# The S5 output of a hybrid layer, made with tokens on partitions and its skip term as a diagonal matmul

## The chip, the core and the metric

The kernel runs on one core of a Trainium2 chip. The time is device time in microseconds for one execution; given are the median of three runs and, for reading, one execution taken with the hardware profiler.

The core's engines are named as in the profile: PE is TensorE (PEld its weight loads), DVE is VectorE, ACT is ScalarE, POOL is GpSimd, SP issues most of the DMAs. Each runs its own instructions in order and waits on semaphores for the others.

## What is computed

Input `x` is 8 batches of 512 tokens with 128 features, all in float32. Four blocks follow each other, each with a layer norm ahead and a residual: a selective state-space block (S6, 256 inner channels with 64 states each), a mixture of experts (8 experts, top 2), an S5 block, and the same mixture of experts again. The change lies in the S5 block:

```python
Lambda_bar = jnp.exp(Lambda * step)
B_bar = ((Lambda_bar - 1.0) / Lambda)[:, None] * B_tilde
Bu = jnp.einsum('blh,ph->blp', u.astype(jnp.complex64), B_bar)
_, xs = jax.lax.associative_scan(combine, (A, Bu), axis=1)
ys = jnp.einsum('blp,hp->blh', xs, C_tilde).real + D * u
...
x = x + _L0_attn_b_ref(_layernorm(x, axis=-1), ...)
```

`u` is the normalized input, `D` one skip factor for each of the 128 features, and there are 64 complex states.

## The kernel before

The kernel handles one batch of 512 tokens at a time. The costly part is S6: 256 channels by 64 states are 128 tiles of 128 rows by 512 tokens. For each tile ACT makes a decay `da` (line 837), POOL the product `w` (line 947, two tiles at a time), DVE runs the scan `h` (line 1251), and PE sums the states (line 633, four tiles at a time). `da` has a ring of 2 pairs, `w` of 5, `h` of 6, so each engine can be only so far ahead of the next.

A **turn** is 128 slots, one scan each. Into the scans of batch b every engine weaves other work at slots written out by hand in `PE_STEPS`: `pre` (norm and projections of batch b+1), `post` (S6's output, the first mixture, S5 and the beginning of the second mixture of batch b-1) and `late` (the rest of the second mixture of batch b-2). Within a slot the scan's work comes first, then `late`, `post`, `pre`. A step's lag behind its PE slot is written with it on each engine. The first pass makes batch 0 ready, then there are eight turns, and a last pass without scans for what is left over. In the text they are counted from 0: turn 0 has no `post`, turn 7 no `pre`.

Three PSUM banks H, G and Y serve all the woven work. A step claims its bank by waiting until the one before it in that bank was drained.

S5 of one batch goes through these steps; all tiles have features, states or tokens on the 128 partitions:

- `uT`, slot 83: the normalized tokens are transposed on PE and copied to `nT` (features by tokens).
- `P1`, `P2`, slot 85: two matmuls of 512 columns into H and Y. DVE turns them by cosine and sine, scans (line 1220), and turns them back into `zt[0]` (line 1223, slot 89) and `zt[1]` (line 1225, slot 90), which are states by tokens and which the trace calls `tq`. The second drains P2.
- `s5`, slot 92, bank H: two matmuls (lines 611 and 613) with the output matrices `mc` as the stationary operand and `zt` as the moving one give features by tokens. The first starts once `zt[0]` is there.
- The skip, slot 93 on DVE (line 1228): `nT` times the feature's factor `sdt` plus the bank, into `yT`, which the trace calls `sq`. It drains s5.
- `s5t`, slot 95, bank Y: four transpositions back to tokens by features; at slot 96 DVE adds them to `x1` into `x2` (line 1233); at slot 97 the moments for the last norm follow (lines 1097 and 1100).

Beside this the next batch's projections run: `dt1`, slot 94 (line 521), goes into bank H. ACT takes it at slot 97 (lines 750 and 751), and after a table load an exponential and a logarithm (lines 754 to 759) DVE makes `dl` from it (line 1120, slots 100 and 101), which SP stores and loads back spread out for the next turn.

Of the kernel before, what the change touches and what calls it, by code (L numbers as in the profile page):

```python
# [91 lines left out]
def weigh_slot(m, e, n):  # L92
# [12 lines left out]
MATRICES_AT = PRE_AT + 11  # L105
TURN_AT = PRE_AT + 18
SCALE_AT = 52
LN_AT = [PRE_AT - 6, 7, 16, S5_AT, MOE_AT[2] - 8]
RSTD_LAG, NORM_LAG = 6, 6
ROUTE = 14  # L110
FIRST_LOADS, PROJECTION_LOADS, LATE_LOADS, EXPERT_LOADS = 6, 13, 12, 3
# [4 lines left out]
PE_STEPS = [  # L116
    (5, "post", "Y", "z"), (MOE_AT[1] - 2, "post", "Y", "x1T"), (MOE_AT[1], "post", "Y", "lg1"),
    (S5_AT + 6, "post", "Y", "uT"), (S5_AT + 8, "post", "H", "P1"), (S5_AT + 8, "post", "Y", "P2"),
    (S5_AT + 15, "post", "H", "s5"), (S5_AT + 18, "post", "Y", "s5t"),
    (MOE_AT[2] - 2, "post", "Y", "x3T"), (MOE_AT[2], "post", "Y", "lg2"),  # L120
] + [(PRE_AT + _n, "pre", _b, _name) for _n, _b, _name in (
    (0, "H", "xnT"), (2, "G", "in0"), (3, "H", "in1"), (7, "G", "in2"), (8, "H", "in3"), (11, "G", "stepsB"),
# [100 lines left out]
def hybrid_kernel(nc, x, Wi, bi, Wx, bx, Wdt, bdt, A_log, Dp, Wo, bo, gamma, beta, Lre, Lim, SB, SC, SD, log_step,  # L223
# [3 lines left out]
    with ExitStack() as ctx:  # L227
        def sb(name, shape, dt=F32):
            return ctx.enter_context(nc.sbuf_tensor(name, shape, dt))
# [15 lines left out]

        s5p = sb("s5p", [128, 3]); s5w = sb("s5w", [128, 32]); s5i = sb("s5i", [128, 1], I32)
        mb = sb("mb", [128, 2, 128]); mc = sb("mc", [128, 2, 128])
        cosT = sb("cosT", [128, L]); sinT = sb("sinT", [128, L]); rT = sb("rT", [128, L]); sdt = sb("sdt", [128, 1])

        xnew = sb("xnew", [128, TT, D]); xn = sb("xn", [128, TT, D]); xnT = sb("xnT", [128, L])  # L250
        th = sb("th", [128, 2, L]); vh = sb("vh", [128, 2, L]); spa, du, dl = th, th, vh
# [12 lines left out]
        sbt, sct = z[0:NS, 0:2, :].rearrange("p a c -> p (a c)").rearrange("p (h j) -> p h j", j=2), z[:, 2, :].rearrange("p (n j) -> p n j", j=2)  # L264
        bb, cc = nrm[0:NS, :, :], x1[:, 0:2, :].rearrange("p j (c n) -> p j c n", c=2)
        zt = [tq[:, 0, :], tq[:, 1, :], sq[:, 0, :], sq[:, 1, :]]
        yT = zt[2]

        banks = {n: ctx.enter_context(nc.psum_tensor("bank" + n, [128, 512], F32)) for n in "HGY"}
        da = [ctx.enter_context(nc.psum_tensor(f"da{j}", [128, 2, 512], F32)) for j in range(D_RING)]  # L270
# [180 lines left out]
        def _(pe):  # L451
# [5 lines left out]
            def is_filled(t, name, ins):  # L457
                ins.then_inc(filled[BANK[name]], 1)

            def turn_tiles(t, name, src):  # L460

                p = claim(t, name)
                for a in range(TT):
                    ins = nc.tensor.transpose(p[:, a * 128:(a + 1) * 128], src(a), ident[:, :])
                is_filled(t, name, ins)
# [117 lines left out]
            def post(t):  # L583
                c = t.b - 1
                yield SLOT["z"]
                p = claim(t, "z")
                pe.wait_ge(direct_ready, 2 * c + 2)
                for a in range(TT):
                    for k in range(2):
                        nc.tensor.matmul(p[:, a * 128:(a + 1) * 128], xd[:, k, a * 128:(a + 1) * 128], wo[:, k, :],  # L590
                                         start=(a == 0 and k == 0), stop=False)
                pe.wait_ge(ys_taken, 2 * c + 2)
                for a in range(TT):
                    for k in range(2):
                        ins = nc.tensor.matmul(p[:, a * 128:(a + 1) * 128], y3[:, k, a * 128:(a + 1) * 128], wo[:, k, :],
                                               start=False, stop=(a == TT - 1 and k == 1))
                is_filled(t, "z", ins)
                yield from moe(t, 1, False)
                yield SLOT["uT"]
                pe.wait_ge(normed[3], 4 * c + 4)  # L600
                turn_tiles(t, "uT", lambda a: nrm[:, a, :])
                yield SLOT["P1"]
                for k, name in enumerate(("P1", "P2")):
                    p = claim(t, name)
                    if k == 0:
                        pe.wait_ge(drained[BANK["uT"]], t.before("uT") + 1)
                    is_filled(t, name, nc.tensor.matmul(p[:, :], mb[:, k, :], nT[:, :], start=True, stop=True))
                yield SLOT["s5"]
                p = claim(t, "s5")
                pe.wait_ge(real_ready, c + 1)  # L610
                nc.tensor.matmul(p[:, :], mc[:, 0, :], zt[0], start=True, stop=False)
                pe.wait_ge(drained[BANK["P2"]], t.before("P2") + 1)
                is_filled(t, "s5", nc.tensor.matmul(p[:, :], mc[:, 1, :], zt[1], start=False, stop=True))
                yield SLOT["s5t"]
                pe.wait_ge(drained[BANK["s5"]], t.before("s5") + 1)
                turn_tiles(t, "s5t", lambda a: yT[:, a * 128:(a + 1) * 128])
                yield from moe(t, 2, False)

            def late(t):
# [336 lines left out]
        def _(v):  # L956
# [11 lines left out]
            def link(ins):  # L968

                step[0] += 1  # L970
                ins.then_inc(setup_chain, 1)
# [34 lines left out]
            def diagonal_setup():  # L1006
# [66 lines left out]
                while n < L:  # L1073
# [10 lines left out]
                    c_, c_next, s_, s_next = c_next, c_, s_next, s_  # L1084
                    n *= 2
                link(V.tensor_scalar(rT[:, :], cosT[:, :], 0.0, er, ALU.mult, ALU.add))
                v.wait_ge(matrices_turned, 1)
                link(V.tensor_copy(mb[:, :, :].rearrange("p n c -> p (n c)"), banks["Y"][:, 0:256]))
                link(V.tensor_copy(mc[:, :, :].rearrange("p n c -> p (n c)"), banks["Y"][:, 256:512]))
# [101 lines left out]
            def post(t):  # L1191
# [31 lines left out]
                V.tensor_tensor(zt[0], p2[:, :], cosT[:, :], ALU.mult).then_inc(real_ready, 1)  # L1223
                yield SLOT["P1"] + 5
                drain("P2", V.tensor_tensor(zt[1], p2[:, :], sinT[:, :], ALU.mult))
                yield SLOT["s5"] + 1
                p = got(t, "s5")
                drain("s5", V.scalar_tensor_tensor(yT[:, :], nT[:, :], sdt[:, 0:1], p[:, :], ALU.mult, ALU.add))
                yield SLOT["s5t"] + 1
                p = got(t, "s5t")  # L1230
                if not known(c, 1):
                    v.wait_ge(x_out, 16 * c)
                drain("s5t", V.tensor_tensor(flat(x2), flat(x1), p[:, :], ALU.add))
                v.wait_ge(drained[BANK["s5t"]], t.before("s5t") + 1)
                yield from moments(4, c, LN_AT[4], x2)
                yield from both(moe_tiles(t, 2, False), routing(t, 2))

# [55 lines left out]
```

## Time and profile before

| | before |
|---|---|
| median of 3 runs | 1848.97 us (1846.12 to 1856.43) |
| the profiled execution | 1861.63 us |
| its span, first to last instruction | 1859.7 us |
| mean granted PE clock | 0.860 of 2.4 GHz |
| scan instructions of DVE (line 1251) | 1024 |

The profiled execution is one more run of the same program, and its times are those of the rows. A row of the timeline gives the start, the duration, the engine, line, operation and tiles, how many instructions it merges, and in brackets how long the engine stood idle before it and what released it. A PE row's end is modelled and can lie behind the start of the next row. The granted clock is 1.0 at 2.4 GHz and 0.5 at 1.2 GHz.

### The profile page before, as it was taken

What the parts mean: (1) busy time and instruction counts of PE and PEld (TensorE: products, weight loads), DVE (VectorE), ACT (ScalarE), POOL (GpSimd) and SP (SyncE); (2) the same over time, 40 slices, a digit from 0 to 9 for tenths busy, and PEclk for the clock granted to TensorE, in tenths of its full rate; (3) what the DMA queues carried; (4) which work ended last, traced back from release to release, by engine and by line L of the source; (5) the groups of instructions that cost most, each with busy time, mean ns of one, the idle gap of its engine ahead of it and who ended that gap; (6) DMA issues with size and microseconds to landing.
All of it is one profiled execution on the core that took longest, in us unless ns stands there. A gap on an engine that the chain in (4) does not pass through costs nothing.

```text
span 1859.7 us, 19053 instructions
## 1 busy us (share of the span) xinstructions
PE 1351.0 (73%) x5928; PEld 617.7 (33%) x5928; DVE 1514.5 (81%) x2105; ACT 1281.5 (69%) x2275; POOL 1513.9 (81%) x888
## 2 busy tenths in 40 slices
PE   4336458777886887778776878778787778668958
PEld 1001123234342343324342343324332343324535
DVE  4879988898889889898899888888888988895222
ACT  4547668687877778777777778777787777755423
POOL 0899999978998799977998899987998799983312
PEclk9557569889987989879897989879898898979979
DMA  3601411122111311132101401132111321100000
GB/s 87 212 34 71 164 46 51 49 91 97 57 40 48 148 51 33 54 104 96 55 25 50 162 29 51 49 106 81 51 51 49 102 85 52 46 29 1 7 1 6
DMA packets 38747, 121.89 MB, mean 66 GB/s; under 512 B 5875, under 2 KB 21110, under 8 KB 26358
## 3 DMA queue, kind: packets, MB, share of 16 engines
q1 hardware_dynamic: 37062, 120.67, 18.3%
q8 instruction: 47, 0.77, 0.2%
q14 instruction: 54, 0.44, 0.1%
q10 hardware_dynamic: 1584, 0.01, 0.0%
HBM read 109.13 MB, written 11.53 MB: 65 GB/s over the span
## 4 chain that ended last, share of the span: by engine, by line
PE 27%; ACT 18%; DVE 15%; POOL 14%; issue 8%; DVEq 0%; POOLq 0%; ACTq 0%
DVE h L1251 10%; POOL w L947 9%; PE bankH L565 8%; ACT da L837 5%; PE bankY L579 5%; PE bankG L565 5%; ACT yk L798 4%; ACT L837 3%; PE ys L633 2%; POOL x L890 2%; PE bankG L512 2%; DVE aq L1189 1%; PE bankY L559 1%; ACT L785 1%; ACT sq L785 1%
## 5 line engine op out<-in xcount | busy, mean ns | idle before, releaser
L1251 DVE TENSOR_TENSOR_SCAN h<-da,w 128x512 f32<-128x512 f32 x1024 | 1192.1, 1206 | 158.3 <-ACT da L837 133.0
L947 POOL TENSOR_TENSOR w<-ur,br 128x1024 f32<-128x1024 f32 x512 | 1193.6, 2365 | 33.1 <-DVE h L1251 21.2
L837 ACT ACTIVATE da<-dr,al 128x511 f32<-128x511 f32 x1024 | 681.9, 687 | 221.9 <-DVE h L1251 212.5
L633 PE MATMUL ys<-h,wsum 128*32 128x512 f32 x2048 | 320.9, 703 | 208.5 <-DVE h L1251 189.2
L565 PE MATMUL bankH<-nT,w 128*128 128x512 f32 x512 | 301.8, 673 | 89.7 <-DVE aq L1189 85.3
L890 POOL TENSOR_TENSOR x<-x,yk 128x512 f32<-128x512 f32 x128 | 163.1, 1274 | 211.2 <-ACT yk L798 210.6
L579 PEld LDWEIGHTS bankY<-w,aq 128*128 128x128 f32 x2048 | 262.8, 203 | 87.0 <-issue 65.0
L579 PE MATMUL bankY<-w,aq 128*128 128x128 f32 x2048 | 270.5, 289 | 12.4 <-DVE aq L1189 7.9
L565 PE MATMUL bankG<-nT,w 128*128 128x512 f32 x432 | 243.8, 648 | 24.6 <-DVE aq L1189 24.6
L798 ACT ACTIVATE yk<-bankY,rt 128x128 f32<-128x128 f32 x512 | 151.8, 364 | 121.5 <-PE bankY L579 107.8
L633 PEld LDWEIGHTS ys<-h,wsum 128*32 128x32 f32 x2048 | 42.9, 115 | 408.5 <-DVE h L1251 373.2
L565 PEld LDWEIGHTS bankH<-nT,w 128*128 128x128 f32 x512 | 87.0, 205 | 243.5 <-DVE aq L1189 147.9
L565 PEld LDWEIGHTS bankG<-nT,w 128*128 128x128 f32 x432 | 80.1, 203 | 163.9 <-issue 89.0
L512 PE MATMUL bankG<-xs,wx 128*128 128x512 f32 x64 | 44.3, 829 | 38.5 <-DVE sres L1115 37.7
L1189 DVE TENSOR_TENSOR aq<-tq,bankH 128x512 f32<-128x512 f32 x64 | 42.7, 667 | 35.3 <-PE bankH L565 35.3
L785 ACT ACT_TABLE_LOAD x55 | 70.6, 1283 | 1.0
L837 ACT ACT_TABLE_LOAD x54 | 69.3, 1283 | 1.0
L1189 DVE TENSOR_TENSOR aq<-tq,bankG 128x512 f32<-128x512 f32 x64 | 42.5, 665 | 32.2 <-PE bankG L565 32.1
L699 ACT ACTIVATE nrm<-x,nm,rs 128x128 f32<-128x128 f32 x96 | 39.4, 480 | 31.5 <-POOL nm L858 31.5
L852 POOL TENSOR_TENSOR var<-bag,eps 128x4 f32<-128x4 f32 x40 | 8.5, 212 | 59.0 <-DVE bag L1100 59.0
L785 ACT ACTIVATE tq<-bankH 128x512 f32<-128x512 f32 x64 | 38.3, 599 | 25.2 <-PE bankH L565 24.9
L785 ACT ACTIVATE sq<-bankH 128x512 f32<-128x512 f32 x64 | 38.2, 597 | 23.2 <-PE bankH L565 23.2
(187 smaller groups left out, 1135.8 us busy)
## 6 DMA issues: line engine op xcount, KB each, us to landing
br<-b_rows SPq DMA_DIRECT2D x64, 1024.0 KB, 5.0
dr<-d_rows SPq DMA_DIRECT2D x16, 1024.0 KB, 7.1
ur<-u_rows SPq DMA_DIRECT2D x16, 1024.0 KB, 8.4
d_rows<-vh SPq DMA_DIRECT2D x16, 256.0 KB
u_rows<-th SPq DMA_DIRECT2D x16, 256.0 KB
xnew<-in_L_attn_a_x_dram SPq DMA_DIRECT2D x8, 256.0 KB, 5.3
w<-in_L_ffn_W_dram SPq DMA_DIRECT2D x2, 1024.0 KB, 11.1
x<-in_L_attn_a_x_dram SPq DMA_DIRECT2D x8, 256.0 KB, 9.1
```

The costliest lines, as they stand in the source:

```text
L512: ins = nc.tensor.matmul(p[:, :], lhs(k), xs[:, k, :], start=(k == 0), stop=(k == 1))
L565: is_filled(t, f"{name}{m}_{n}", nc.tensor.matmul(p[:, :], wt[:, n // 2, n % 2 * 128:n % 2 * 128 + 128], nT[:, :], start=True, stop=True))
L579: ins = nc.tensor.matmul(p[:, a * 128:(a + 1) * 128], aq[:, (2 * n + k) % 4, a * 128:(a + 1) * 128], w3[:, n, k, :], start=(k == 0), stop= ...
L633: ins = nc.tensor.matmul(ys[32 * q:32 * q + 32, :], wsum[:, :], h[:, (DUOS * t.b + 2 * group + q // 2) % H_RING, q % 2, :], start=(n == 0) ...
L699: A(dst[:, a, :], src[:, a, :], ACT.Identity, bias=nm[:, k, a:a + 1], scale=rs[:, k, a:a + 1]).then_inc(normed[k], 1)
L785: A(zt[j % 4], p[:, :], ACT.Silu).then_inc(drained[BANK[f"h{m}_{j}"]], 1)
L798: ins = A(yk[:, a, :], p[:, a * 128:(a + 1) * 128], ACT.Copy, scale=rt[:, 0, a, e:e + 1])
L837: A(da[duo % D_RING][:, k % 2, 1:L], dr[:, half, q, 1:L], ACT.Exp, scale=nega[:, QUADS * half + q, n:n + 1]).then_inc(decay_ready, 1)
L890: G.tensor_tensor(total[:, :, :], total[:, :, :], yk[:, :, :], ALU.add).then_inc(added, 1)
L947: G.tensor_tensor(w[:, turn_duo % W_RING, :, :], ur[:, half, q:q + 2, :], br[:, chunk % B_RING, row:row + 1, :].to_broadcast([128, 2, L]), ...
L1189: drain(f"g{m}_{n}", V.tensor_tensor(aq[:, n % 4, :], zt[n % 4], p[:, :], ALU.mult))
L1251: V.tensor_tensor_scan(h[:, turn_duo % H_RING, k % 2, :], da[duo % D_RING][:, k % 2, :], w[:, turn_duo % W_RING, k % 2, :], 0.0, ALU.mult, ...
```

## The change

S5's output is now made directly as tokens by features. For each 128 tokens PE takes the slice of `nT` as the stationary operand and a 128x128 diagonal matrix `dskip` of the skip factors as the moving one, then the slices of `zt[0]` and `zt[1]` with the two halves of `mc`, all accumulated in a quarter of bank Y. That is 12 matmuls of 128x128 in place of 2 of 128x512 and 4 transpositions. The DVE skip op is gone, and the addition into `x2` reads bank Y. `dskip` is made once, in the setup. `s5` stays at slot 92 but moves from bank H to Y, the addition moves from slot 96 to 94, and the moments from 97 to 96.

```diff
-LN_AT = [PRE_AT - 6, 7, 16, S5_AT, MOE_AT[2] - 8]
+LN_AT = [PRE_AT - 6, 7, 16, S5_AT, MOE_AT[2] - 9]
...
-    (S5_AT + 15, "post", "H", "s5"), (S5_AT + 18, "post", "Y", "s5t"),
+    (S5_AT + 15, "post", "Y", "s5"),
...
                 p = claim(t, "s5")
                 pe.wait_ge(real_ready, c + 1)
-                nc.tensor.matmul(p[:, :], mc[:, 0, :], zt[0], start=True, stop=False)
-                pe.wait_ge(drained[BANK["P2"]], t.before("P2") + 1)
-                is_filled(t, "s5", nc.tensor.matmul(p[:, :], mc[:, 1, :], zt[1], start=False, stop=True))
-                yield SLOT["s5t"]
-                pe.wait_ge(drained[BANK["s5"]], t.before("s5") + 1)
-                turn_tiles(t, "s5t", lambda a: yT[:, a * 128:(a + 1) * 128])
+                for a in range(TT):
+                    cols = slice(a * 128, (a + 1) * 128)
+                    nc.tensor.matmul(p[:, cols], nT[:, cols], dskip[:, :], start=True, stop=False)
+                    for k in range(2):
+                        ins = nc.tensor.matmul(p[:, cols], zt[k][:, cols], mc[:, k, :], start=False, stop=(k == 1))
+                is_filled(t, "s5", ins)
...
+                link(V.tensor_scalar(dskip[:, :], ident[:, :], sdt[:, 0:1], None, ALU.mult))
...
-                yield SLOT["s5"] + 1
+                yield SLOT["s5"] + 2
                 p = got(t, "s5")
-                drain("s5", V.scalar_tensor_tensor(yT[:, :], nT[:, :], sdt[:, 0:1], p[:, :], ALU.mult, ALU.add))
-                yield SLOT["s5t"] + 1
-                p = got(t, "s5t")
                 if not known(c, 1):
                     v.wait_ge(x_out, 16 * c)
-                drain("s5t", V.tensor_tensor(flat(x2), flat(x1), p[:, :], ALU.add))
-                v.wait_ge(drained[BANK["s5t"]], t.before("s5t") + 1)
+                drain("s5", V.tensor_tensor(flat(x2), flat(x1), p[:, :], ALU.add))
+                v.wait_ge(drained[BANK["s5"]], t.before("s5") + 1)
```

PE's order in turn 1, from the sums at slot 90 on, before: lines 611 and 613 are s5, 521 is dt1, and the transpositions of `sq` are s5t.

```order
L633 MATMUL ys<-h,wsum 32x512 x4
L611 MATMUL bankH<-tq,mc 128x512
L613 MATMUL bankH<-tq,mc 128x512
L633 MATMUL ys<-h,wsum 32x512 x4
L521 MATMUL bankH<-steps_and_b,wdt 128x512
L464 MATMUL bankY<-ident,sq 128x128 x4
L633 MATMUL ys<-h,wsum 32x512 x8
L464 MATMUL bankY<-ident,nrm 128x128 x4
```

The same place now; a line number is one lower where code was taken out above it, and the two rows of S5 stand four times, once for each 128 tokens.

```order
L632 MATMUL ys<-h,wsum 32x512 x4
L612 MATMUL bankY<-dskip,nT 128x128
L614 MATMUL bankY<-mc,tq 128x128 x2
...
L632 MATMUL ys<-h,wsum 32x512 x4
L520 MATMUL bankH<-steps_and_b,wdt 128x512
L632 MATMUL ys<-h,wsum 32x512 x8
L463 MATMUL bankY<-ident,nrm 128x128 x4
```

S5 fills another bank with twelve short matmuls, dt1 keeps its place behind the same sums, and nothing stands between it and the next sums.

DVE's order at the same place before: line 1225 makes `zt[1]`, 1228 is the skip, 1233 the addition.

```order
L1225 TENSOR_TENSOR tq<-bankY,sinT 128x512
L1251 SCALAR_TENSOR_TENSOR h<-da,w 128x512 x3
L1228 SCALAR_TENSOR_TENSOR sq<-nT,sdt,bankH 128x512
L1251 SCALAR_TENSOR_TENSOR h<-da,w 128x512 x3
L1233 TENSOR_TENSOR x<-x,bankY 128x512
L1251 SCALAR_TENSOR_TENSOR h<-da,w 128x512
L1097 BN_STATS bst<-x 128x6 x4
L1100 BN_AGGR bag<-bst 128x2 x4
L1251 SCALAR_TENSOR_TENSOR h<-da,w 128x512 x3
L1120 TENSOR_TENSOR vh<-th,bankG 128x512
```

And now, where the scan is line 1248 and the addition line 1230:

```order
L1225 TENSOR_TENSOR tq<-bankY,sinT 128x512
L1248 SCALAR_TENSOR_TENSOR h<-da,w 128x512 x4
L1230 TENSOR_TENSOR x<-x,bankY 128x512
L1248 SCALAR_TENSOR_TENSOR h<-da,w 128x512 x2
L1097 BN_STATS bst<-x 128x6 x4
L1100 BN_AGGR bag<-bst 128x2 x4
L1248 SCALAR_TENSOR_TENSOR h<-da,w 128x512 x4
L1120 TENSOR_TENSOR vh<-th,bankG 128x512
```

The skip is gone, the addition comes two scans earlier and the moments one; the first `dl` op (line 1120) stands behind the same ten scans.

## Rows read from the trace of the kernel before

**Rows 1.** The page: busy time by engine, and the chain that ended last

```profile
PE 1351.0 (73%) x5928; PEld 617.7 (33%) x5928; DVE 1514.5 (81%) x2105; ACT 1281.5 (69%) x2275; POOL 1513.9 (81%) x888
PE 27%; ACT 18%; DVE 15%; POOL 14%; issue 8%; DVEq 0%; POOLq 0%; ACTq 0%
```

**Rows 2.** Windows, turn 4: stretch, length, busy PE, PEld, DVE, ACT, POOL, clock, DMA

```profile
859.00:1071.00 212.00, 164.47 (x740) 76.79 (x740) 186.53 (x249) 161.73 (x287) 188.50 (x110) 0.90 0.19 69
```

**Rows 3.** Pieces of the chain that ended last: start us, us, what

```profile
756.51 3.58 PE bankY L579 x16
862.18 1.79 PE bankY L595 x16
1056.34 1.80 PE bankY L579 x16
1073.89 1.79 PE bankY L595 x16
1288.75 1.79 PE bankY L595 x16
```

**Rows 4.** Line 1228: durations in ns, and who waited for it (us, times)

```profile
L1228 DVE SCALAR_TENSOR_TENSOR sq<-nT,sdt,bankH x8: 715/718/748, 370.1 to 1797.5; 128x512 f32<-128x512 f32 x8
  PEld bankH L521: 16.3, 6
```

**Rows 5.** Timeline of DVE, turn 4: start us, us, engine, line, operation

```profile
1004.40 0.66 DVE L1225 TENSOR_TENSOR tq<-bankY,sinT 128x512 f32<-128x512 f32 x1
...
1008.34 0.72 DVE L1228 SCALAR_TENSOR_TENSOR sq<-nT,sdt,bankH 128x512 f32<-128x512 f32 x1
1008.98 3.44 DVE L1251 TENSOR_TENSOR_SCAN h<-da,w 128x512 f32<-128x512 f32 x3
1012.34 0.66 DVE L1233 TENSOR_TENSOR x<-x,bankY 128x512 f32<-128x512 f32 x1
...
1015.35 3.50 DVE L1251 TENSOR_TENSOR_SCAN h<-da,w 128x512 f32<-128x512 f32 x3
1018.77 0.66 DVE L1120 TENSOR_TENSOR vh<-th,bankG 128x512 f32<-128x512 f32 x1
```

**Rows 6.** Timeline of PE, same stretch; in brackets idle before, and releaser

```profile
1001.12 1.06 PE L633 MATMUL ys<-h,wsum 128*32 128x512 f32 x8
1003.49 1.10 PE L611 MATMUL bankH<-tq,mc 128*128 128x512 f32 x2 [1.31 <-DVE tq L1223]
1005.11 1.12 PE L613 MATMUL bankH<-tq,mc 128*128 128x512 f32 x2 [0.52 <-DVE tq L1225]
1006.24 1.06 PE L633 MATMUL ys<-h,wsum 128*32 128x512 f32 x8
1009.11 2.01 PE L521 MATMUL bankH<-steps_and_b,wdt 64*128 64x512 f32 x2 [1.80 <-DVE sq L1228]
```

**Rows 7.** Windows of PE alone: stretch, length, busy (instructions), granted clock, DMA, GB/s

```profile
886.00:890.00 4.00, 1.15 (x9) 0.97 0.00 0
890.00:893.00 3.00, 3.00 (x14) 0.50 0.02 5
968.00:972.00 4.00, 4.00 (x24) 0.57 0.00 0
972.00:975.00 3.00, 2.14 (x11) 1.00 0.00 0
```

**Rows 8.** Timeline of ACT, turn 4

```profile
1011.16 0.69 ACT L750 ACTIVATE th<-bankH,bdts 128x512 f32<-128x512 f32 x1 [2.01 <-PE bankH L521]
...
1016.93 2.50 ACT L837 ACTIVATE da<-dr,al 128x511 f32<-128x511 f32 x4
```

**Rows 9.** Timeline of all engines, the last pass

```profile
1793.53 0.68 DVE L1225 TENSOR_TENSOR tq<-bankY,sinT 128x512 f32<-128x512 f32 x1
...
1797.55 0.75 DVE L1228 SCALAR_TENSOR_TENSOR sq<-nT,sdt,bankH 128x512 f32<-128x512 f32 x1 [3.34 <-PE bankH L613]
...
1799.05 0.69 DVE L1233 TENSOR_TENSOR x<-x,bankY 128x512 f32<-128x512 f32 x1 [0.75 <-PE bankY L464]
```

More of the change, by code:

```diff
@@ L247, in hybrid_kernel @@
         mb = sb("mb", [128, 2, 128]); mc = sb("mc", [128, 2, 128])
-        cosT = sb("cosT", [128, L]); sinT = sb("sinT", [128, L]); rT = sb("rT", [128, L]); sdt = sb("sdt", [128, 1])
+        cosT = sb("cosT", [128, L]); sinT = sb("sinT", [128, L]); rT = sb("rT", [128, L]); sdt = sb("sdt", [128, 1]); dskip = sb("dskip", [128, 128])
         xnew = sb("xnew", [128, TT, D]); xn = sb("xn", [128, TT, D]); xnT = sb("xnT", [128, L])
@@ L266, in hybrid_kernel @@
         zt = [tq[:, 0, :], tq[:, 1, :], sq[:, 0, :], sq[:, 1, :]]
-        yT = zt[2]
         banks = {n: ctx.enter_context(nc.psum_tensor("bank" + n, [128, 512], F32)) for n in "HGY"}
```

## The prediction

> **What bounds the kernel now.** I read the page first [rows 1]: VectorE (DVE) and GpSimd (POOL) are both busy 81% of the span, and the chain that ended last passes through all four engines, so no single engine's sum gives the time. Next the busy times of one whole middle turn, 859 to 1071 us [rows 2]: DVE 186.5 and POOL 188.5 of 212 us. A turn is a pass over one batch's 128 scans with the previous batches' other work woven in; it leaves each of these engines about 25 us idle, so what one instruction is worth depends on where it stands. The length of a turn is the distance between two equal pieces of the chain [rows 3]: from 862.18 to 1073.89 it is 211.7 us, from there to 1288.75 it is 214.9 us, with the same instructions. Of the five such distances between 435.6 and 1500.5 us, three are 211.7 and two 214.9.
>
> Then the place of the change. The DVE instruction that goes (line 1228) takes 0.72 us, eight times, and the matmuls of line 521 into bank H waited for it 16.3 us in six turns, 2.7 us each [rows 4]. That matmul is dt1, the last projection of the next batch. It had to wait because S5's result lay in bank H, and it sat second in line behind it. The reader should see next whether DVE itself has a hole there. It has none: in the turn I use throughout, from 1004.40 to 1018.77 us each DVE row starts where the one before ends [rows 5]. The last row but one there shows three scans in 3.50 us where the others take 3.44, so ScalarE's (ACT) decays reach DVE with nothing to spare at that point.
>
> **What goes.** The skip op costs DVE the distance from its start to the next one, 1008.34 to 1008.98, 0.64 us [rows 5]. In seven turns it lies in a packed stretch, so if nothing else comes late its removal is worth 7 x 0.64 = 4.5 us. In the last pass, which has no scans, it stands in a serial chain and is counted there. The four transpositions run on TensorE (PE) behind dt1; their removal only frees PE.
>
> **What comes on PE.** S5's output was two matmuls of 512 columns, the first at 1003.49 while DVE still made the second operand, the second at 1005.11 [rows 6]. Now there are twelve matmuls of 128x128, all behind the claim of bank Y, which waits until DVE has drained P2, that is until the second operand is there: 1004.40 + 0.66 = 1005.06. None can start earlier, although the diagonal one needs only nT. Their price is that of the expert outputs, which have the same shapes: 8 matmuls, 16 instructions in the trace, take 1.80 us at 1056.34 and 3.58 us at 756.51, where the clock is the lower one [rows 3]. Twelve are 24 instructions: 2.70 us at 2.4 GHz, 5.37 us at 1.2 GHz. The second old matmul took about 0.9 us before the sums at 1006.24 could start. The Trainium skill, "TensorE: Matmul & The Clock Gate", section "Back-to-back issue gap", gives about 81 ns for a load and matmul of 128 columns; by it the 24 would take 1.9 us. The trace's 1.80/16 = 0.11 us disagrees, and I use the trace.
>
> **Which clock.** Before, PE ran the first S5 matmul inside the pause between the sums that end at 1002.18 and the second matmul at 1005.11 [rows 6]. Without it PE does nothing for 2.9 us. The trace has a like place: in 886 to 890 us PE did 1.15 us of work, and from 890 to 893 its clock was granted at 0.50 [rows 7]. So I expect the clock to fall to 1.2 GHz just after S5's matmuls start. It comes back under dense work: in 968 to 972 PE was busy throughout at a mean of 0.57, and 972 to 975 is at 1.00 [rows 7]. There one expert group of 16 instructions went by before the clock was up, so I let 15 of S5's 24 run at the lower clock and 9 at the higher: 15 x 0.224 + 9 x 0.1125 = 4.4 us. Bounds are 2.7 and 5.4. The Trainium skill says the same against this change, on the same page, section "Loop structure matters more than you think": whether matmuls stay warm is set by the loop, and long waits between them make PE run cold. The rows agree that a thin stretch precedes a fall.
>
> **What that does to dt1, and to ACT.** On PE dt1 now waits for no DVE op, only for its place: S5 from 1005.11, 4.4 us; the sums, whose row has 1.06 with an end that overlaps what follows, 0.9; dt1 1.1 as the other pair of 512 columns at 2.4 GHz [rows 6]: it ends at 1011.5. Before it ended at 1009.11 + 2.01 = 1011.12. ACT was idle 2.01 us for it [rows 8] and then runs dt1's two passes, a table load, exponential and logarithm between the decays; the decays at 1016.93 follow in order. They were already just in time for DVE's three scans at 1015.35. So ACT is 0.38 us later and DVE, although it has 0.64 us less to do, waits about 1.0 us for decays: the turn gets 0.38 us longer. Queued behind that wait on DVE are the two dl ops from 1018.77 and the next scans; behind these come the stores of the next batch. Six turns contain dt1: 6 x 0.38 = +2.3 us.
>
> **The rest.** The addition into x2 moves from slot 96 to 94 and now waits for S5 directly. With S5 done at about 1009.6 and the scan ahead of it ending at about 1009.5 it waits some 0.2 us, which the later wait for ACT swallows. If S5 took 5.4 us it would wait 1.0 us. The moments and what follows stand one slot earlier; on ACT the normalization passes one decay (2.50/4 = 0.6 us [rows 8]), whose scan comes only after two more and the dl ops: nothing, with 0.6 us as the bound. The seventh turn has no dt1: 0, between -0.6 and +0.6. In the last pass everything is serial [rows 9]: from the second operand's end, 1794.21, to the end of the addition, 1799.74, it is 5.53 us, part at each clock. Now it is 4.4 + 0.2 + 0.69 = 5.3: -0.2, with 2.7 + 0.9 = 3.6 (-1.9) and 5.4 + 0.9 = 6.3 (+0.8) as bounds. The diagonal is made once, 128x128, a quarter of the skip op's size: +0.2, between 0 and 0.7, on a DVE that waits in the setup anyway.
>
> Sum: +2.3 + 0 - 0.2 + 0.2 = +2.3 us. The profiled execution took 1861.63 us (span 1859.7); it would be 1864. It lies 0.7% above the median of the runs, 1848.97, and I carry the difference over: **1851 us**.
>
> **Rivals.** *The clock holds, and DVE's op is simply gone.* S5 takes 2.7 us, dt1 ends at 1005.11 + 2.7 + 0.9 + 1.1 = 1009.8, ACT is 1.3 us early and DVE sets the pace: -4.5 - 1.9 + 0.2 = -6.2, 1843 us. For it: PE is dense ahead of the pause. Against it: 2.9 us of idle PE.
>
> *dt1 becomes the bound (slower).* If all of S5, the sums and dt1 run at 1.2 GHz, they take 5.4 + 2 x 0.9 + 2.0 = 9.2 us, dt1 ends at 1014.3, 3.2 us later than before, and ACT and DVE with it: 6 x 3.2 = 19.2, and with the upper bounds of the last pass and the diagonal (0.8 + 0.7) +20.7, 1870 us. It decides from the point at which dt1 ends over 6.0 us behind the second operand (1011.12 - 1005.06). Against it: so dense a stretch raised the clock at 968.
>
> *The pattern of turns changes.* The same work takes 211.7 or 214.9 us a turn [rows 3], and shifting each turn by some tenths may choose otherwise. If all five are long: +2.3 + 3 x 3.15 = 1861 us; if all are short: +2.3 - 2 x 3.15 = 1845 us. Only the sizes speak for it; nothing in the rows says which way.
>
> That the op does not disappear is no rival: the order has no DVE instruction between the scans there.
>
> **How the numbers follow.** Forecast 0.50, clock holds 0.22, dt1 bound 0.08, long turns 0.12, short turns 0.08. About 0.5% (9.2 us) is what a measurement of this kernel can tell from no change. Faster by more, below 1839.7, only if short turns and a holding clock meet, or a gain that I have missed: 0.09. Slower by more, above 1858.2: the dt1 case and most of the long turns, 0.16. Within: 0.75. Range 1840 to 1862, which leaves out the dt1 case and takes in the spread of the runs before.
>
> **What would show it.** In the new profile: no line 1228; bank Y's S5 matmuls in one group of 24 lasting 4 to 4.6 us, with a granted clock under 1 in it; dt1 ending 6.0 to 6.7 us after the second operand; DVE idle about 1 us before the scans that follow, released by ACT's decays; turns of about 212 us. A group of 2.7 us and no such idle time would put the clock step wrong; a dt1 over 8 us behind would put the recovery wrong.

## The result, and the profile after

The changed kernel takes 1863.02 us (median of 14 runs, 1856.63 to 1869.14). The kernel before, run beside it, takes 1853.24 us (14 runs, 1846.12 to 1864.26). The ratio is 1.005 with a 95% interval of 1.003 to 1.007: the change makes the kernel slower by 5.6 to 13 us, where the forecast was +2.3 us. The profiled execution after took 1861.51 us (span 1859.6), almost exactly as long as that of before (1861.63). The two spans say nothing of the change, because the profiled run of before lies 8 us above the median of its 14. So I compare stretches of a turn, which repeat six or seven times inside each trace.

The page after, with the first line of [rows 1]. DVE has seven instructions fewer (eight skip ops, less the diagonal) and 4.3 us less to do. The chains that ended last can't be compared: in this trace it can be followed back only to 1393 us, in that of before to 328.

```profile
PE 1342.9 (72%) x6056; PEld 635.1 (34%) x6056; DVE 1510.2 (81%) x2098; ACT 1281.3 (69%) x2275; POOL 1514.6 (81%) x888
```

Now the place of the change in turn 4. The timeline of PE (start us, us, engine, line, operation; in brackets idle before and releaser), which answers to [rows 6]:

```profile
1004.78 0.49 PE L612 MATMUL bankY<-dskip,nT 128*128 128x128 f32 x2 [2.93 <-DVE tq L1225]
...
1009.29 1.06 PE L632 MATMUL ys<-h,wsum 128*32 128x512 f32 x8
1010.28 1.12 PE L520 MATMUL bankH<-steps_and_b,wdt 64*128 64x512 f32 x2
```

PE is idle for 2.93 us until the second operand is there, at 1004.07 + 0.67 = 1004.74. S5's 24 instructions then take until about 1009.4, 4.6 us behind the operand. dt1, two instructions of 512 columns, ends at 1010.28 + 1.12 = 1011.40, 6.7 us behind the operand; before, it was 6.06.

ACT's row that waits for dt1 in this turn, as [rows 8]; the idle time has grown from 2.01 to 2.63 us:

```profile
1011.44 0.69 ACT L749 ACTIVATE th<-bankH,bdts 128x512 f32<-128x512 f32 x1 [2.63 <-PE bankH L520]
```

DVE in the same turn, as [rows 5]:

```profile
1004.07 0.67 DVE L1225 TENSOR_TENSOR tq<-bankY,sinT 128x512 f32<-128x512 f32 x1
1004.65 4.56 DVE L1248 TENSOR_TENSOR_SCAN h<-da,w 128x512 f32<-128x512 f32 x4
1009.40 0.69 DVE L1230 TENSOR_TENSOR x<-x,bankY 128x512 f32<-128x512 f32 x1 [0.19 <-PE bankY L614]
...
1016.27 1.22 DVE L1248 TENSOR_TENSOR_SCAN h<-da,w 128x512 f32<-128x512 f32 x1 [0.42 <-ACT da L836]
1017.92 1.22 DVE L1248 TENSOR_TENSOR_SCAN h<-da,w 128x512 f32<-128x512 f32 x1 [0.42 <-ACT da L836]
1019.06 0.66 DVE L1120 TENSOR_TENSOR vh<-th,bankG 128x512 f32<-128x512 f32 x1
```

The skip op is gone, and DVE waits instead: 0.19 us at the addition, and twice 0.42 us for decays at the scans from 1016.27 on. (A wait costs about 0.1 us more than its bracket, because scans in a row overlap: one takes 1.22 us, four take 4.56.) I measure the net effect by the **piece**: the time from the start of the second operand (line 1225) to the start of the first dl op (line 1120). Both stand in every trace, with the same scans between them in nearly all of the kernels below. In turn 4 of before it is 1018.77 - 1004.40 = 14.37 us [rows 5], here 1019.06 - 1004.07 = 14.99.

Turn 3 after is worse. Rows of PE, DVE and ACT there, in order of time:

```profile
787.24 0.67 DVE L1225 TENSOR_TENSOR tq<-bankY,sinT 128x512 f32<-128x512 f32 x1
...
787.96 0.79 PE L612 MATMUL bankY<-dskip,nT 128*128 128x128 f32 x2 [2.93 <-DVE tq L1225]
...
793.48 0.69 DVE L1230 TENSOR_TENSOR x<-x,bankY 128x512 f32<-128x512 f32 x1 [1.10 <-PE bankY L614]
...
794.71 1.12 PE L520 MATMUL bankH<-steps_and_b,wdt 64*128 64x512 f32 x2
...
795.87 0.69 ACT L749 ACTIVATE th<-bankH,bdts 128x512 f32<-128x512 f32 x1 [3.89 <-PE bankH L520]
...
803.49 0.66 DVE L1120 TENSOR_TENSOR vh<-th,bankG 128x512 f32<-128x512 f32 x1
```

S5 takes 5.5 us here, dt1 ends 7.9 us behind the operand, ACT waits 3.89 us, and the piece is 803.49 - 787.24 = 16.25 us. Windows of PE alone show why the turns differ: stretch, length, busy (instructions), granted clock, DMA share and GB/s. The first row is turn 4's pause, the next two its S5, the two after them turn 5's S5, and the last one turn 3's:

```profile
1002.00:1004.70 2.70, 0.00 (x0) 1.00 0.45 185
1004.80:1005.70 0.90, 0.90 (x8) 1.00 0.00 0
1005.80:1009.10 3.30, 3.30 (x18) 0.50 0.00 0
1217.50:1220.70 3.20, 3.20 (x15) 0.50 0.00 0
1220.90:1221.90 1.00, 1.00 (x10) 1.00 0.00 0
788.00:793.30 5.30, 5.30 (x24) 0.50 0.01 3
```

In turn 3 every one of the 24 instructions ran at 1.2 GHz. In turn 4 the first eight still ran at 2.4 GHz, and in turn 5 the last nine did; by their starts, sixteen and fifteen of the 24 ran at 1.2 GHz there. The same for every turn that has a dt1, in us ("behind the operand" counts from the second operand's end); the last column is the sum of its six pieces:

| kernel | S5's end behind the operand | dt1's end behind the operand | piece | sum of the pieces |
|---|---|---|---|---|
| before | (two matmuls) | 5.2 to 6.06 | 14.29 14.28 14.29 14.37 14.28 14.31 | 85.82 |
| after | 4.63 4.57 5.54 4.63 4.57 5.55 | 6.68 6.62 7.93 6.68 6.62 7.93 | 15.00 14.94 16.25 14.99 14.95 16.25 | 92.38 |

The six turns lose 92.38 - 85.82 = 6.56 us at this place.

### The profile page after: what moved, and what is told of

It reads as the page before. It is cut to its first block and busy times, and to the rows that moved or that the text cites. A ratio compares the mean times of both kernels' runs of the same rounds, so it can differ in the third digit from the quotient of the medians.

```text
span 1859.6 us, 19294 instructions
## 1 busy us (share of the span) xinstructions
PE 1342.9 (72%) x6056; PEld 635.1 (34%) x6056; DVE 1510.2 (81%) x2098; ACT 1281.3 (69%) x2275; POOL 1514.6 (81%) x888
## 5 line engine op out<-in xcount | busy, mean ns | idle before, releaser
L836 ACT ACTIVATE da<-dr,al 128x511 f32<-128x511 f32 x1024 | 681.5, 687 | 219.2 <-DVE h L1248 209.7
L632 PE MATMUL ys<-h,wsum 128*32 128x512 f32 x2048 | 311.9, 685 | 215.7 <-DVE h L1248 196.4
L578 PEld LDWEIGHTS bankY<-w,aq 128*128 128x128 f32 x2048 | 254.6, 198 | 86.2 <-issue 64.1
L578 PE MATMUL bankY<-w,aq 128*128 128x128 f32 x2048 | 262.0, 283 | 12.5 <-DVE aq L1189 7.9
L564 PE MATMUL bankG<-nT,w 128*128 128x512 f32 x432 | 248.5, 659 | 24.6 <-DVE aq L1189 24.6
L784 ACT ACTIVATE tq<-bankG 128x512 f32<-128x512 f32 x64 | 38.1, 595 | 24.1 <-PE bankG L564 23.4
```

The costliest lines, as they stand in the source:

```text
L564: is_filled(t, f"{name}{m}_{n}", nc.tensor.matmul(p[:, :], wt[:, n // 2, n % 2 * 128:n % 2 * 128 + 128], nT[:, :], start=True, stop=True))
L578: ins = nc.tensor.matmul(p[:, a * 128:(a + 1) * 128], aq[:, (2 * n + k) % 4, a * 128:(a + 1) * 128], w3[:, n, k, :], start=(k == 0), stop= ...
L632: ins = nc.tensor.matmul(ys[32 * q:32 * q + 32, :], wsum[:, :], h[:, (DUOS * t.b + 2 * group + q // 2) % H_RING, q % 2, :], start=(n == 0) ...
L784: A(zt[j % 4], p[:, :], ACT.Silu).then_inc(drained[BANK[f"h{m}_{j}"]], 1)
L836: A(da[duo % D_RING][:, k % 2, 1:L], dr[:, half, q, 1:L], ACT.Exp, scale=nega[:, QUADS * half + q, n:n + 1]).then_inc(decay_ready, 1)
```

## The experiments

The theory after the result, called A: S5 at a low clock pushes dt1 past the point from which it sets the end of the piece, and nothing else of the change costs time. Rival B: the addition into x2, which stands earlier now and waits directly for S5, costs the time. Rival C: the difference comes from the turns' lengths as a whole, not from this place.

**Second profiles of both kernels.** No edit; is what the first traces show a property of the kernels?

> The kernel before, unchanged, for a second profile: the first profiled execution (1861.63 us) was 8 us above the median of its runs. Theory (a small lengthening of slots 92 to 103 decides between turns of 211.7 and about 215 us): slots 92 to 103 take 17.1 us again, and an execution near the median of 1853 us has no or one long turn among turns 2 to 6. Rival (the executions differ elsewhere, in the setup or the last pass): the turns are the same as in the first profile, and first scan or last pass differ by several us.

> The changed kernel, unchanged, for a second profile. Theory: slots 92 to 103 take 17.8 to 19.1 us in the six turns with dt1, as S5 ends 4.5 to 5.5 us behind its second operand, and turns of 212.2 to 215.3 us. Rival: S5 ends near 3 us in most turns here, and the first profile was an exception.

The single times beside each other were 1853.89 and 1858.41 us. The pieces of before were 14.29 to 14.33 us in all six turns again. Those of after were 14.70, 16.25, 14.99, 14.99, 14.72 and 16.26: two bad turns of six as in the first profile, though in turns 2 and 6 now where it was 3 and 6. The turns of before differ between its two profiles, as the chain shows (second profile; start us, us, what):

```profile
852.38 2.05 PE bankY L590 x16
1067.30 2.05 PE bankY L590 x16
1279.01 2.05 PE bankY L590 x16
```

They are 214.92 and 211.71 us apart. This one is the only long turn of the five here; in [rows 3] there were two. That explains some of the spread between runs of one kernel, and why one pair of spans can mislead. A long turn of before loses its time between its scans 4 and 92 (149.6 us where a short one takes 146.5), not at the place of the change.

**Keep PE busy in the pause (e1_filler).** Four instructions ahead of S5's claim, into bank H, whose result nobody reads:

```
+                if t.pre:
+                    pe.wait_ge(drained["H"], t.before("dt1"))
+                    for k in range(2):
+                        nc.tensor.matmul(banks["H"][:, :], mb[:, k, :], nT[:, :], start=True, stop=True)
                 p = claim(t, "s5")
```

> The changed kernel, with two more matmuls of 512 columns (those of P1 and P2 again, into bank H once it is free; nobody reads the result) on TensorE in the pause ahead of S5's twelve. Theory (the pause lets the clock fall inside S5, S5 takes 4.5 to 5.5 us, dt1 and with it ScalarE come late): with the pause filled the clock stays at 2.4 GHz, the S5 group takes 2.7 to 3.0 us, dt1 ends about 5 us behind the second operand, and the time is 0 to 6 us below the kernel before (ratio 0.997 to 1.000). Rival (the pattern of long and short turns alone made the difference, not the place of the change): ratio stays near 1.005. Second rival (it is not the clock but the number of TensorE instructions): the S5 group stays over 4 us and the ratio at 1.005 or above.

Measured: 1853.06 us, ratio 1.0007 (0.9992 to 1.0022). PE in turn 4:

```profile
994.10 1.98 PE L611 MATMUL bankH<-nT,mb 128*128 128x512 f32 x4
997.10 0.49 PE L616 MATMUL bankY<-dskip,nT 128*128 128x128 f32 x2 [1.02 <-DVE tq L1229]
...
1000.97 1.12 PE L520 MATMUL bankH<-steps_and_b,wdt 64*128 64x512 f32 x2
```

DVE in the same turn; from operand to dl op there is no idle time in brackets:

```profile
996.38 0.66 DVE L1229 TENSOR_TENSOR tq<-bankY,sinT 128x512 f32<-128x512 f32 x1
...
1005.56 4.53 DVE L1252 TENSOR_TENSOR_SCAN h<-da,w 128x512 f32<-128x512 f32 x4
1010.01 0.66 DVE L1124 TENSOR_TENSOR vh<-th,bankG 128x512 f32<-128x512 f32 x1
```

S5 ends 3.0 us behind the operand in all six turns, dt1 ends 5.05 us behind the operand, and the piece is 13.63 us, 0.66 less than before: the price of the skip op. The whole loss of the change is gone with a few instructions in PE's pause, and the interval excludes that of after. This speaks for A and against C. But the gain that the pieces promise, 6 x 0.66 = 4 us against before, does not show in the time. The other experiments come back to that.

**dt1 ahead of S5 (e2_dt1_first).** With S5 in bank Y, dt1's bank H is free earlier:

```
-    (24, "H", "dt1")
+    (21, "H", "dt1")
```

> The changed kernel with one number changed: dt1, and all that follows it by lag, stands at slot 91 in place of 94, so on TensorE it runs ahead of S5's twelve matmuls, inside the pause. Theory (dt1 behind the longer S5 is what costs): ScalarE gets dt1 several us earlier, no decay is late for the scans at slots 96 to 100, the only thing left is VectorE's own wait for S5 at the addition (0 to 1 us a turn); ratio 0.996 to 1.001. Rival (pattern of turns): ratio near 1.005. Rival (VectorE's direct wait for S5 at the addition is the whole cost, dt1 is covered): 0.9 to 1.3 us a turn stay, ratio 1.003 to 1.005.

Measured: 1853.31 us, ratio 1.001 (0.9993 to 1.0027). PE in turn 4:

```profile
993.13 1.12 PE L520 MATMUL bankH<-steps_and_b,wdt 64*128 64x512 f32 x2
996.13 0.49 PE L612 MATMUL bankY<-dskip,nT 128*128 128x128 f32 x2 [1.88 <-DVE tq L1225]
```

S5 is as slow as in the four better turns of after (4.63 us in five turns), since PE still pauses ahead of it. But dt1 is done before the operand is there, and the loss is gone. So it isn't the slow S5 as such that costs, but dt1 behind it: A, not B. (The dl ops stand earlier here, so the piece can't be compared.)

**The addition back at its old place (e3_late_add).** Two slots later, so that DVE never waits for S5:

```
-LN_AT = [PRE_AT - 6, 7, 16, S5_AT, MOE_AT[2] - 9]
+LN_AT = [PRE_AT - 6, 7, 16, S5_AT, MOE_AT[2] - 8]
-                yield SLOT["s5"] + 2
+                yield SLOT["s5"] + 4
```

> The changed kernel with the addition back at slot 96 and the moments back at 97. Theory (dt1 and ScalarE are late): VectorE no longer waits for S5 at the addition, but waits for decays as long as before; ratio 1.003 to 1.005. Rival (the addition was put too early and its direct wait is the cost): the wait is gone and VectorE keeps the 0.64 us of the removed op; ratio 0.997 to 1.000.

Measured: 1859.06 us, ratio 1.003 (1.0013 to 1.0047). DVE in turn 3, where after had waited 1.10 us at the addition:

```profile
795.65 0.66 DVE L1230 TENSOR_TENSOR x<-x,bankY 128x512 f32<-128x512 f32 x1
```

The row has no bracket: the wait at the addition is gone. But the pieces are the same as in after: 16.26, 14.98, 14.99, 14.73, 16.25, 14.98 us. The time that DVE no longer spends waiting for S5 it spends waiting for decays a few scans later. B falls.

**The bank alone (e4_bank_only).** In the kernel before, S5's result goes into bank Y; the skip op and the transpositions stay:

```
-    (S5_AT + 15, "post", "H", "s5"), (S5_AT + 18, "post", "Y", "s5t"),
+    (S5_AT + 15, "post", "Y", "s5"), (S5_AT + 18, "post", "Y", "s5t"),
```

> The kernel before with S5's two matmuls in bank Y in place of H, nothing else: the first of them then waits for the second operand too, and dt1 no longer waits for the skip op. Theory (clock and length of S5 decide): the pause makes the clock fall, but four instructions of 512 columns take only 1.7 to 3.7 us, dt1 ends 5.2 to 6.0 us behind the second operand, no later than before; ratio 0.998 to 1.002. Rival (any move of the order shifts the pattern of turns to the longer one): ratio near 1.005.

Measured: 1857.54 us, ratio 1.0031 (1.0013 to 1.005), slower than I expected. Its profile shows one bad turn of six, the first. PE there:

```profile
363.33 1.91 PE L613 MATMUL bankY<-tq,mc 128*128 128x512 f32 x2
...
367.04 1.42 PE L521 MATMUL bankH<-steps_and_b,wdt 64*128 64x512 f32 x2
```

dt1 ends 7.05 us behind the operand and the piece is 15.36 us. In the other five it ends at 5.7 us and the piece is 14.29, as before. One turn's 1.1 us is not 0.3% of the time, which is 5.7 us. The profiled execution (1854.78) is one of the shorter ones of its 12, so others may have had more bad turns; that is not shown, and the rest of this ratio stays open.

**Without the diagonal (e5_no_diag).** S5's output without the skip D*u, which this kernel leaves out: 16 instructions instead of 24.

```
-                    nc.tensor.matmul(p[:, cols], nT[:, cols], dskip[:, :], start=True, stop=False)
...
-                        ins = nc.tensor.matmul(p[:, cols], zt[k][:, cols], mc[:, k, :], start=False, stop=(k == 1))
+                        ins = nc.tensor.matmul(p[:, cols], zt[k][:, cols], mc[:, k, :], start=(k == 0), stop=(k == 1))
```

> The changed kernel without the four diagonal matmuls, so the skip term D*u of S5 is left out of the result; S5 is 8 matmuls (16 instructions) in place of 12. Theory (the length of S5 on TensorE carries through dt1 to ScalarE and the decays): the clock still falls in it, but the group ends 3.2 to 3.8 us behind the second operand, dt1 5.2 to 5.8 us, no later than in the kernel before, and slots 92 to 103 take 16.5 to 17.1 us; ratio 0.999 to 1.002. Rival (any twelve-fold order in bank Y loses its time elsewhere, by the pattern of turns): ratio near 1.005.

Measured: 1851.99 us, ratio 0.9981 (0.9964 to 0.9999). PE in turn 4:

```profile
999.24 3.42 PE L613 MATMUL bankY<-mc,tq 128*128 128x128 f32 x16 [2.93 <-DVE tq L1224]
...
1003.59 1.12 PE L520 MATMUL bankH<-steps_and_b,wdt 64*128 64x512 f32 x2
```

Same pause of 2.93 us, and 3.42 us for 16 instructions: 0.21 us each, nearly all at 1.2 GHz ([rows 3] give 3.58 us for sixteen there). S5 is short enough all the same: dt1 ends at 5.5 us, and the piece is 13.84.

**The kernels above on one line.** The piece follows dt1's end, turn by turn, whatever made dt1 late:

| dt1's end behind the operand | piece | where |
|---|---|---|
| 5.05 | 13.63 | e1, all turns |
| 5.52 | 13.84 | e5 |
| 5.72 | 14.29 (with the skip op) | e4, five turns |
| 5.2 to 6.06 | 14.28 to 14.37 (with it) | before |
| 6.40 | 14.72 | after, second profile |
| 6.68 | 14.99, 15.00 | after |
| 7.05 | 15.36 | e4, turn 1 |
| 7.93 | 16.25 | after |

The piece is dt1's end plus 8.3 us, or DVE's own work if that is longer: 13.63 us without the skip op and 14.29 with it. They cross at 5.3 and 6.0 us. So the change can only gain at this place where dt1 ends within 6.0 us of the operand, and gains all of the 0.66 us only within 5.3. As it is made, dt1 ends 2.05 us or more behind S5's end, and S5 would have to end within 3.9 us of the operand to gain anything.

**What DVE's time is worth (e6_skip_twice).** The kernel before with the skip op done twice, the first time into a tile that is written over:

```
+                V.scalar_tensor_tensor(zt[3], nT[:, :], sdt[:, 0:1], p[:, :], ALU.mult, ALU.add)
                 drain("s5", V.scalar_tensor_tensor(yT[:, :], nT[:, :], sdt[:, 0:1], p[:, :], ALU.mult, ALU.add))
```

> The kernel before with VectorE's skip op run twice, the second time into an unused tile: the price of what the change removes. Theory (VectorE is packed there, but what is won or lost on it is made good by the clock's rise at the start of the second mixture): slots 92 to 103 get 0.5 to 0.7 us longer, turns grow by 0 to 0.4 us, ratio 0.999 to 1.002. Rival (a VectorE op costs its full time in each turn): 0.64 us x 7 + 0.75 = 5.2 us, ratio 1.003.

Measured: 1867.77 us, ratio 1.0084 (1.0061 to 1.0107); neither expectation holds. The same group of PE in two successive turns, from the timeline:

```profile
863.37 2.05 PE L590 MATMUL bankY<-wo,xd 128*128 128x128 f32 x16 [1.54 <-ACT yk L798]
...
1078.41 2.05 PE L590 MATMUL bankY<-wo,xd 128*128 128x128 f32 x16 [1.54 <-ACT yk L798]
```

The piece grows by 0.66 us (14.95), as it must. dt1 is not the reason: it ends 5.83 us behind the operand, no later than before. But the turns are 215.04 us apart where most of before are 211.7. Counted from scan start to scan start, the first four scans of turn 4 take 11.0 us here and 8.17 in before, and scans 108 to 111, beside the expert mixture, 9.92 and 9.13; 0.9 us of this is won back between scans 4 and 92. PE's clock was low at the first of these places, where it is high in before. Windows of PE around the start of turn 4, the first row in e6 (851.79), the second in before (851.39):

```profile
848.00:856.70 8.70, 6.00 (x13) 0.61 0.96 381
848.00:856.70 8.70, 6.41 (x32) 1.00 0.95 377
```

So rival C's mechanism exists: 0.66 us more at this place, and turns 2 to 6 all take 213.9 to 215.0 us. In after, whose pieces are as long or longer, it did not happen: its turns 2 and 5 take 212.2 us, 0.5 more than the short ones of before, 3 and 6 take 214.2, and 4 takes 215.3, 0.5 more than the long ones of before. Why the same delay costs so much more in e6 is not shown.

**Why a gain does not show.** In e1 turns 2 to 6 are all the same length (chain of e1):

```profile
853.97 1.79 PE bankY L594 x16
1065.60 1.79 PE bankY L594 x16
```

They are 211.63 us apart, and so are the others; the short turns of before have 211.7. DVE is 0.66 us ahead behind the piece, and loses it again: 0.3 to 0.5 us at scans 108 to 111, beside the mixture (9.59 us, where before has 9.13 to 9.31), and 0.2 us between scans 4 and 92. PE's logits there, in e1 and, second fence, in before, each with windows on either side of the clock's rise (the columns are those of the windows above):

```profile
1014.81 1.88 PE L558 MATMUL bankY<-wg,nT 128*128 128x8 f32 x8 [2.27 <-ACT nT L664]
...
1018.80:1021.80 3.00, 3.00 (x5) 0.50 0.73 279
1021.90:1024.90 3.00, 3.00 (x14) 1.00 0.98 325
```

```profile
1023.57 1.88 PE L559 MATMUL bankY<-wg,nT 128*128 128x8 f32 x8 [1.39 <-ACT nT L661]
...
1026.60:1029.60 3.00, 3.00 (x4) 0.50 1.00 343
1029.70:1032.70 3.00, 3.00 (x14) 1.00 0.62 229
```

In e1 the logits start 1014.81 - 996.38 = 18.4 us behind the operand's start, in before 1023.57 - 1004.40 = 19.2. The clock is up 25.5 us behind it in e1 and 25.3 in before. So the mixture is asked for 0.7 us earlier and gets its full clock no earlier. The turns of e5, with a piece of 13.84 us, are 211.6 us long as well, and so are those of e2, with the slow S5. What holds the turn at this length in kernels that win time at different places is not shown.

**Warm matmuls ahead of the mixture (e8_warm on e1, e9_warm_before on before).** Six fillers, one a slot, behind S5:

```
+                for n in range(6):
+                    yield SLOT["s5"] + 5 + n
+                    if t.pre:
+                        pe.wait_ge(drained["Y"], t.before("s5") + 1)
+                        nc.tensor.matmul(banks["Y"][:, :], mb[:, 0, :], nT[:, :], start=True, stop=True)
```

> The kernel with the filled pause (e1_filler) and six more matmuls of 512 columns into bank Y at slots 97 to 102, whose results nobody reads, one a slot, so that TensorE is busy up to the second mixture. Theory (the 0.66 us that the filled pause won at slots 92 to 103 was given back at slots 108 to 111, because the second mixture starts at 1.2 GHz and the clock rises at the same distance from the turn's start): the clock is 2.4 GHz from the mixture's start, slots 104 to 127 get 1 to 3 us shorter, ratio 0.990 to 0.996. Rival (it was given back to something else, GpSimd or ScalarE): slots 104 to 127 stay at 37.5 to 37.9 us and the ratio at 1.000; the sums that stand behind the added matmuls could then cost up to 1 us a turn.

> The kernel before, with the same six matmuls at slots 97 to 102 and nothing else changed. Theory: the same 1 to 3 us a turn are won in slots 104 to 127, and the kernel with the change and both fillers is 0 to 0.7 us a turn ahead of this one; ratio 0.991 to 0.997. Rival as for e8_warm: ratio 1.000.

Measured: e8 1849.78 us, ratio 0.9989 (0.9974 to 1.0004); e9 1849.23 us, ratio 0.9978 (0.9962 to 0.9993). Both fell short, for different reasons. Windows of PE in e8, ahead of the mixture and into it; the clock is high while the fillers run and low again just when the mixture starts:

```profile
1009.00:1014.60 5.60, 2.60 (x13) 0.92 0.18 47
1014.70:1021.40 6.70, 6.70 (x14) 0.57 0.65 221
```

In e9 the clock stays up there, and the scans 108 to 111 take 7.15 us instead of 9.13. But then it is low at the start of the next turn, and the first four scans take 9.82 us instead of 8.17. The turn's length is again 211.6 us. A window of e9 there:

```profile
837.70:840.50 2.80, 2.80 (x7) 0.50 1.01 427
```

**Fillers at both places (e10_warm_all on e8, e11_warm_all_before on e9).** Two matmuls more at the last logits, and two in the last two slots of a turn:

```
+        if m == 2 and name == "lg" and t.pre:
+            pe.wait_ge(drained["H"], t.before("h2_0"))
+            for k in range(2):
+                nc.tensor.matmul(banks["H"][:, :], mb[:, k, :], xnT[:, :], start=True, stop=True)
...
+                for n in range(2):
+                    yield PAIRS - 2 + n
+                    if t.pre:
+                        pe.wait_ge(drained["G"], t.before("g2_6") + 1)
+                        nc.tensor.matmul(banks["G"][:, :], mb[:, n, :], xnT[:, :], start=True, stop=True)
```

> The changed kernel with the filled pause and the six added matmuls of e8_warm, two more into bank H ahead of the second mixture's logits and two into bank G at slots 126 and 127, all in the six middle turns and read by nobody. They stand where TensorE idled ahead of a stretch that then ran at 1.2 GHz in e8_warm and e9_warm_before. Theory (the clock takes back what VectorE wins): the second mixture's start and the turn's start run at 2.4 GHz, slots 108 to 111 take 7.2 us, slots 0 to 3 8.2 us, 92 to 103 16.5 us; turns of 208 to 210 us, ratio 0.988 to 0.994. Rival (turns stay at 211.6 us whatever is won in one place, since something else takes it): ratio 0.998.

> The kernel before with the same added matmuls but the one that fills S5's pause, which it does not have. Theory: the same gain but for VectorE's 0.66 us a turn, so 3 to 5 us more than e10_warm_all; ratio 0.990 to 0.996. Rival: the removed VectorE op is worth nothing even here, both alike.

Measured: e10 1839.82 us (1828.75 to 1848.02), ratio 0.9939 (0.9915 to 0.9964), faster than both kernels. A window of PE over the last 59 us of its turn 4 and the first 3 of the next, in which the clock never falls:

```profile
988.00:1050.00 62.00, 53.33 (x238) 1.00 0.35 129
```

The three places came out as expected (scans 108 to 111 in 7.15 us, the first four in 8.17, 92 to 103 in 16.46), but scans 4 to 91 take 145.7 to 152.0 us from turn to turn. Its turns are 208.1 to 214.4 us, five of them 1053.1 together, where e1 takes 1058.1. The profiled run is one of its longer ones (1847.37), so what its best runs look like is not shown.

e11, the same fillers with the kernel before, takes 1863.68 us, ratio 1.0076 (1.0052 to 1.01), where I expected a gain. Its profiled execution is its fastest (1846.46) and its turns are short as well (209.7 to 213.4). What the others lose is not in that trace, and stays open.

## Why the prediction was wrong

**The mechanism: right.** The idle 2.9 us of PE, the fall of the clock in S5, dt1's lateness, ACT's idle time in front of it and DVE's wait for decays are all there, in that order and at the places named. e1 shows that the pause causes the slow S5 (3.0 us without it), e2 that it costs only through dt1. "It decides from the point at which dt1 ends over 6.0 us behind the second operand" holds: in the table above, every dt1 beyond 6.0 us gives a piece over the 14.29 us of before, one for one.

**The step that failed: the size of S5, and so of dt1's term.** I took one value for all six turns, "15 x 0.224 + 9 x 0.1125 = 4.4 us", and so 0.38 us a turn, +2.3 us in all. Measured, S5 ends 4.6 us behind the operand in four turns, which lose 0.6 to 0.7 us each, and 5.5 us in two, which lose 1.96. That is 6.6 us in the first profile and 6.1 in the second (91.91 - 85.81), not 2.3. Of the 4.3 us that are missing in the first, the two bad turns make 3.2 and the four others 1.1.

In the four turns the count of fifteen was right: by the instructions' starts it was fifteen or sixteen. e1 has all 24 instructions at 2.4 GHz and S5's end at 3.0 us, turn 3 has all at 1.2 GHz and 5.54 us; 4.6 us lies between them as fifteen slow ones of 24 would ((4.6 - 3.0) / (5.54 - 3.0) x 24). What was off there was the price at 2.4 GHz, 2.9 us for the 24 in e1 and not 2.70. In the two bad turns the count was wrong: all 24 ran slowly. The recovery had been read at one place of one turn, and where in S5 the clock falls and rises differs from turn to turn, so a single turn, however typical, could not give the sum. The 5.4 us that I had named as S5's bound went into the addition and the last pass, but I never carried it through dt1 for a part of the turns.

Three readings beside this were off and changed little. The second old matmul kept PE from 1005.11 to 1006.24, 1.13 us and not 0.9. The sums ahead of dt1 took 0.99 us after the change (1009.29 to 1010.28), not 0.9. And the 2.7 us for which dt1 waited on average is the idle time of its weight load (PEld, [rows 4]); in turn 4 PE itself stood idle 1.80 us for it [rows 6].

**How that becomes the time.** With 6.6 us for 2.3 the sum in the first profiles is 6.6 + 0 - 0.2 + 0 = 6.4 us, and in the second ones 6.1 + 0.3 + 0.3 + 0 = 6.7, within the measured 5.6 to 13. In the traces the loss is seen again: turns 2 to 6 together, from first scan to first scan, take 1068.07 and 1067.38 us after, and 1061.68 in the second profile of before, 6.4 and 5.7 us more, with one long turn each; the first profile of before has 1064.87, with two. The medians differ by 9.8 us; the 3.4 us beyond the 6.4 lie inside the interval and have no row.

**What the sum was added to.** The three runs shown had a median of 1848.97; fourteen give 1853.24. The forecast difference on that would have read 1855.5 us. So of the 12 us between the forecast 1851 and the measured 1863.02, 4.3 are the base, about 4 the dt1 term, and the rest has no row.

**The smaller terms: right within their bounds.** The skip op is worth 0.66 us where nothing else is late (e1; I had 0.64). The addition waits 0.19 us in turn 4 and 1.10 in turn 3 (0.2 and 1.0 were forecast). Its line shows 7.8 us in six places; 4.65 of them are the last pass and 0.56 the seventh turn, and what is left is swallowed by the wait for ACT, as e3 shows:

```profile
L1230 DVE TENSOR_TENSOR x<-x,bankY x8: 686/686/689, 367.8 to 1798.8; 128x512 f32<-128x512 f32 x8
  PE bankY L614: 7.8, 6
```

The seventh turn is 205.23 us after and 205.21 before: 0 (205.47 and 205.18 in the second profiles). The last pass, as [rows 9], here after:

```profile
1793.50 0.68 DVE L1225 TENSOR_TENSOR tq<-bankY,sinT 128x512 f32<-128x512 f32 x1
1798.83 0.69 DVE L1230 TENSOR_TENSOR x<-x,bankY 128x512 f32<-128x512 f32 x1 [4.65 <-PE bankY L614]
```

From the operand's end, 1794.18, to the end of the addition, 1799.52, it is 5.34 us, where 5.3 was forecast and 5.53 measured before. That it fits so well is luck: in the second profile of after it is 5.80 us, against 5.54 in that of before, a loss of 0.3 in place of the gain of 0.2. The diagonal in the setup costs nothing that can be seen.

**The rivals.** *The clock holds* is out: it needs S5 at 2.7 us, and S5 took 4.6 and 5.5 us with the clock at 0.50 in most or all of it. Nor would its time have come: e1 has S5 at 3.0 us and DVE's 0.66 us, and is no faster than before. I had priced DVE's gain as time of the run; the turn gave it back, most of it at the mixture. *dt1 becomes the bound* is what happened, by its own criterion. Its price of 3.2 us a turn assumed that the sums and dt1 run at 1.2 GHz too; dt1's 1.12 us in turn 3 is the fast one, and the worst turn costs 1.96. Its chance of 0.08 was for the whole of it, and I had no case in which part of the turns go that way. *The pattern of turns* did not change: both profiles of after have one long turn, those of before two and one. e6 shows that the turns' length can change, for 14 us.

## What to carry to other kernels

Where the trace shows a low clock behind pauses of TensorE, price a group of short matmuls that starts behind such a pause at the low clock for all of it as the bad case, and ask in how many turns it comes; if the sum is then over the slack of the first one who waits, reorder (e2) or fill the pause (e1) before removing another engine's op. Find the slack by the one consumer that decides, here dt1's end against 6.0 us, and look at every turn of the trace, not at one. Time won on a busy engine is only worth what the next meeting point with another engine doesn't wait for anyway.

## What the runs showed of the hardware that I had not expected

- The same program repeats its turns with S5 at 4.6 us in some and 5.5 us in others, and the place changes between two executions (turns 3 and 6, then 2 and 6): where the clock falls and rises is not tied to the program's order alone.
- 0.66 us more on DVE in a turn of 211.7 us cost 14 us (e6, 1.0084), while 0.66 us less gained nothing that can be measured (e1, 1.0007).
- Matmuls whose results nobody reads made the changed kernel 0.6% faster than the kernel before (e10) and the kernel before 0.8% slower (e11).
